# Next batch's input tile by tile, GpSimd's pivot step first, and every loop over batches written out

## The chip, the cores and the metric

One core of one Trainium2 chip runs the whole program in one launch. The metric is the device time of the launch in microseconds, the median of several runs. Engines: TensorE (matmuls), VectorE, ScalarE, GpSimd (POOL) and SyncE (SP), each with its own instruction stream; they meet at semaphores.

## The reference

The input x is (8, 512, 576), the condition (8, 576), all float32:

```
ada = silu(c) @ W_ada + b_ada       # shift, scale, gate for attention and for the MLP
h = layernorm(x) * (1 + scale_msa) + shift_msa
x = x + gate_msa * (softmax(q * 36**-0.5 @ k.T) @ v @ W_proj + b_proj)    # 16 heads of 36
h = layernorm(x) * (1 + scale_mlp) + shift_mlp
x = x + gate_mlp * (gelu(h @ W_fc1 + b_fc1) @ W_fc2 + b_fc2)              # 2304 wide
U, _ = qr(P)                                   # P is (576, 64)
R = expm(skew(silu(c) @ W.T + b))              # one 64x64 rotation a batch
z = x @ U;  out = x + (z @ R - z) @ U.T
```

## The kernel before, in words

A first block loads and splits the weights. Each float32 matrix is held as a rounded high part and a low part, and products are sums of three passes (high x high, high x low, low x high).

The attention block works through the 8 batches, each in 64 numbered slots: 4 slots a head, one for each 128 keys. In slot n TensorE issues the scores for the row maximum of slot n + 10 (L1025), the scores for slot n + 2 (L1041), then the "units" that a hand-written table FIRST_SLOT puts in this slot, then the value products of slot n (L1052, L1053). ScalarE takes two exponentials a slot (phi, L741, and pf, L744), VectorE the row maximum of slot n + 9 (L868) and the low part plo of slot n (L875). The units share two PSUM banks G in turn: `ln` transposes a fifth of the next batch's normalised x (L940), `qk` and `v` are the projections of the next heads, `tr` and `p` transpose and project the output of the batch before, `rv` computes rows of the rotation, and `el` broadcasts a row of the pivot matrix (L1003).

The pivot matrix serves the QR of P: an elimination of 64 steps in batches 0 to 3 and another of 64 in batches 4 to 7, one step for each head. For head h TensorE broadcasts the row (unit el h), VectorE copies it to prow (L856), and GpSimd does the step: `cholesky_step` in batches 0 to 3 (L582 to L593), `sign_step` in batches 4 to 7 (L620 to L635). el h + 1 waits for step h through row_ready. GpSimd does step h in slot 4h + 3.

The next batch's x goes into one tile xln of 4 token tiles, which also holds the residual of the batch before until its rows are stored (L675, for tiles 0 to 3 in slots 13, 20, 24 and 31). GpSimd loads the whole of it in slot 32 (L242). VectorE takes the statistics of tile i in slot 36 + i (L249, L252), GpSimd the inverse root of the variance of all four in slot 39 (L258, L260), VectorE normalises in slots 40 and 41 (L265). TensorE transposes in slots 41 to 45. For the part transposed in slot n, VectorE modulates in slot n + 1 (L813), ScalarE copies the high part in slot n + 2 (L706), and VectorE subtracts for the low part in slot n + 2 (L821), which frees the bank for slot n + 2's transposes.

Within a slot GpSimd's order is: divide the head's output, add and store the residual, load x, invert, load the residual, pick rows for the pivots, pivot step. In slot 39 the inversion thus stands ahead of pivot step 9, which reads what VectorE copied in slot 38, and which el 10 in slot 40 waits for.

Batches -1 (only the preparation of batch 0), 0, 7 and 8 (only the last output) are written out in each engine's stream. Between them run loops with a register for b: on TensorE, VectorE and GpSimd one over batches 1 to 3 and one over 4 to 6, on ScalarE and SyncE one over 1 to 6. Waits in a loop compare with values computed from the register. A third block computes the rotations; the last one, the MLP, works in 16 chunks of 256 tokens, two a batch, with a loop over batches 1 to 6 on every engine.

## Time and profile before

| what | value |
|---|---|
| three runs | 2677.41 us median (2676.99 to 2680.6) |
| the profiled execution | 2683.11 us, span 2681.5 us |
| mean granted TensorE clock | 0.944 of full speed |
| busy share | TensorE 88%, VectorE 53%, ScalarE 41%, GpSimd 29% |
| start | to 128.5 us (el 0 of batch 0) |
| attention, el 0 of batch 0 to the end | 128.5 to 1499 us |
| rotations | 1499 to 1624 us |
| MLP | 1624 to the end |

A span is from the first to the last instruction. A row of a timeline gives start, duration (us), engine, line, operation, what is written and read, and in brackets the idle time before it with what ended it; "issue" means that the profile shows nothing that the engine waited for. A row of windows gives the stretch, its length, then busy time and (x instructions) of TensorE, of its weight loads, of VectorE, ScalarE and GpSimd, the granted TensorE clock as a share of full speed (1.0 is 2.4 GHz, 0.5 is 1.2 GHz), the mean busy share of the DMA engines, and GB/s. Waits give the total in us, how many, and the longest. "el h" is the L1003 of head h, and a window between two of them is taken from start to start.

### The profile page before, as it was taken

The page shows a single profiled execution, that of the slowest core. Times are in us where ns is not written, and L with a number is a line of the kernel's source. Part 1 is how long each engine was busy: PE and PEld are TensorE (multiplying, and loading weights), DVE is VectorE, ACT ScalarE, POOL GpSimd, SP SyncE. Part 2 cuts the span into 40 slices and gives each one's busy share as a digit, 9 for nine tenths or more (in the row PEclk, how much of TensorE's full clock was granted, in tenths as well). Part 3 has the DMA queues.
Part 4 walks back from the last instruction along what each step waited for, and adds up shares of the span by engine and source line. Part 5 has one row for each costly group of instructions (what it writes and reads, how often), then busy time and mean ns, then how long its engine had stood idle before and what let it go on. Part 6 is the DMA issues. An engine that isn't in the chain of part 4 may idle for free. (4 is left out here: it accounts for less than half of the span.)

```text
span 2681.5 us, 49135 instructions
## 1 busy us (share of the span) xinstructions
PE 2365.1 (88%) x15081; PEld 2036.1 (76%) x15081; DVE 1428.6 (53%) x2994; ACT 1098.9 (41%) x2362; POOL 766.5 (29%) x1547
## 2 busy tenths in 40 slices
PE   6698988988889789898997468999999999999998
PEld 1466756756667577576774457999999999999998
DVE  3577676676776767767776473333333333333332
ACT  2265555555555555555655122222222222222221
POOL 1033333343434344334445481111111111111110
PEclk9798999989999899899998688999999999999998
DMA  7122222231322222222221241010101010110100
GB/s 227 38 75 72 56 81 70 64 91 51 88 68 59 72 73 85 70 55 80 72 71 54 70 129 40 28 39 28 39 27 39 28 39 31 35 37 30 36 26 27
DMA packets 99893, 160.53 MB, mean 60 GB/s; under 512 B 23296, under 2 KB 43872, under 8 KB 99616
## 3 DMA queue, kind: packets, MB, share of 16 engines
q1 hardware_dynamic: 86752, 110.35, 14.4%
q0 software_dynamic: 11856, 46.60, 5.3%
q8 instruction: 143, 2.34, 0.4%
q14 instruction: 118, 0.97, 0.1%
q10 hardware_dynamic: 1024, 0.26, 0.0%
HBM read 80.10 MB, written 20.16 MB: 37 GB/s over the span
## 5 line engine op out<-in xcount | busy, mean ns | idle before, releaser
L1653 PE MATMUL bank<-h2T,w 128*128 128x256 f32 x4032 | 531.0, 283 | 9.7 <-issue 6.9
L1653 PEld LDWEIGHTS bank<-h2T,w 128*128 128x128 f32 x4032 | 508.0, 191 | 11.3 <-issue 8.1
L1562 DVE TENSOR_TENSOR glo<-bank,ghi 128x256 fp32r<-128x256 f32 x288 | 122.2, 424 | 688.5 <-ACT bank L1529 688.5
L1666 PE MATMUL bank<-w,ghi 128*128 128x288 f32 x2304 | 476.5, 298 | 0.4
L1528 ACT ACTIVATE ghi<-bank,b 128x256 fp32r<-128x256 f32 x288 | 136.4, 474 | 689.4 <-PE bank L1653 689.4
L875 DVE TENSOR_TENSOR plo<-pf,phi 128x512 fp32r<-128x512 f32 x512 | 365.3, 713 | 89.0 <-ACT pf L744 86.1
L868 DVE TENSOR_REDUCE negm<-bank 128x1 f32<-128x512 f32 x512 | 349.3, 683 | 108.9 <-PE bank L1025 103.6
L1666 PEld LDWEIGHTS bank<-w,ghi 128*128 128x128 f32 x2304 | 367.2, 189 | 2.4 <-DVE x2T L1572 2.0
L741 ACT ACTIVATE phi<-bank 128x512 fp32r<-128x512 f32 x512 | 307.6, 601 | 94.5 <-PE bank L1041 58.8
L1666 PE MATMUL bank<-w,glo 128*128 128x288 f32 x1152 | 340.8, 296 | 0.0
L744 ACT ACTIVATE pf<-bank 128x512 f32<-128x512 f32 x512 | 310.0, 605 | 0.2 <-DVE plo L875 0.2
L960 PE MATMUL bank<-hT,wqk 128*128 128x512 f32 x1008 | 261.5, 399 | 2.9 <-DVE hT L821 2.9
L1052 PE MATMUL bank<-phi,vv 128*73 128x512 f32 x512 | 227.2, 444 | 36.2 <-DVE plo L875 35.4
L1025 PE MATMUL bank<-ks,qs 108*128 108x512 f32 x512 | 235.4, 460 | 18.0 <-issue 11.8
L1041 PE MATMUL bank<-qs,ks 109*128 109x512 f32 x512 | 218.7, 427 | 19.3 <-ACT pf L744 13.0
L960 PEld LDWEIGHTS bank<-hT,wqk 128*128 128x128 f32 x1008 | 192.1, 191 | 47.6 <-DVE hT L821 3.3
L1666 PEld LDWEIGHTS bank<-w,glo 128*128 128x128 f32 x1152 | 216.4, 188 | 0.0
L1053 PE MATMUL bank<-plo,vv 128*73 128x512 f32 x512 | 211.3, 413 | 0.0
L948 PEld LDWEIGHTS bank<-wv,hT 128*128 128x128 f32 x896 | 135.4, 198 | 35.4 <-DVE qklo L833 19.9
L948 PE MATMUL bank<-wv,hT 128*128 128x288 f32 x896 | 147.8, 309 | 11.1 <-DVE qklo L833 10.3
L1502 POOL TENSOR_TENSOR xs<-xs,x2T 128x288 f32<-128x288 f32 x64 | 49.5, 807 | 360.5 <-DVE x2T L1572 360.5
L1025 PEld LDWEIGHTS bank<-ks,qs 108*128 108x128 f32 x512 | 102.2, 200 | 64.7 <-issue 27.0
(222 smaller groups left out, 3300.4 us busy)
## 6 DMA issues: line engine op xcount, KB each, us to landing
xln<-x POOLq DMA_DIRECT2D x16, 1152.0 KB, 6.7
qs<-qkhi SPq DMA_DIRECT2D x192, 72.0 KB
ks<-qkhi SPq DMA_DIRECT2D x192, 72.0 KB
wst<-w_fc POOLq DMA_DIRECT2D x34, 288.0 KB, 3.1
x_d<-xln POOLq DMA_DIRECT2D x32, 288.0 KB, 2.5
xa<-x_d SPq DMA_DIRECT2D x32, 288.0 KB, 2.7
xs<-x_d SPq DMA_DIRECT2D x16, 576.0 KB, 4.0
out<-xs SPq DMA_DIRECT2D x16, 576.0 KB, 2.9
```

What stands on the lines that cost most here:

```text
L741: act.activation(phi[PBUF[n]][:, :], S[n % 2][:, :], ACT.Exp, scale=SCALE).then_inc(exp_hi, 1)
L744: act.activation(pf[n % 2][:, :], S[n % 2][:, :], ACT.Exp, scale=SCALE).then_inc(exp_f, 1)
L868: dve.tensor_reduce(negm[m // TT % 2][:, m % TT:m % TT + 1], M[m % 2][:, :], AX.X, ALU.max, negate=True).then_inc(m_read, 1)
L875: dve.tensor_tensor(plo[PBUF[n]][:, :], pf[n % 2][:, :], f32(phi[PBUF[n]][:, :]), ALU.subtract).then_inc(p_lo, 1)
L948: mm = pe.matmul(G[g_bank(it, u)][:, 0:HALF], hT[0:rows, a, tt * PAR:(tt + 1) * PAR], wv[0:rows, w, half * HALF:(half + 1) * HALF], start= ...
L960: mm = pe.matmul(G[g_bank(it, u)][:, :], wqk[0:rows, w, t * PAR:(t + 1) * PAR], hT[0:rows, a, :], start=first, stop=last)
L1025: pe.matmul(M[m % 2][:, :], qs[h % RING][0:STACK, qt * PAR:(qt + 1) * PAR], ks[h % RING][0:STACK, :], start=True, stop=True).then_inc(m_fu ...
L1041: pe.matmul(S[m % 2][:, :], ks[h % RING][:, kt * PAR:(kt + 1) * PAR], qs[h % RING][:, :], start=True, stop=True).then_inc(s_full, 1)
L1052: pe.matmul(O[0:2 * HD + 1, :], v, phi[PBUF[n]][:, :], start=(kt == 0), stop=False)
L1053: pe.matmul(O[0:2 * HD + 1, :], v, plo[PBUF[n]][:, :], start=False, stop=(kt == TT - 1)).then_inc(pv, 1)
L1653: mm = pe.matmul(F[ft % 2][:, 0:CH], w1[0:rows, w, ft * PAR:(ft + 1) * PAR], h[0:rows, a, :], start=(i == 0), stop=(i == len(FULL_PASSES) ...
L1666: mm = pe.matmul(Y[2 * tt + half][:, 0:HALF], g[ft % 2][:, span], w2[:, ft, w, half * HALF:(half + 1) * HALF], start=(ft == 0 and i == 0), ...
```

## The change

All loops over batches are written out, in the attention block and in the MLP block; waits then compare with constants. x of the next batch is loaded in four transfers, each with its own semaphore and each waiting for the store of its own tile, and statistics, inversion and normalisation are spread over earlier slots. In a slot GpSimd does the pivot step ahead of the inversion and the loads; step 9 moves from slot 39 to slot 38, el 0 from slot 1 to 2, el 11 from slot 47 to 46. Modulate, the high copy and the low subtraction each come one slot earlier relative to their transposes.

```
@@ -86,18 +86,21 @@
               (43, ("ln", 2)), (44, ("ln", 3)), (45, ("ln", 4)), (48, ("qk", 0)), (50, ("v", 0, 0)), (52, ("qk", 1)),
               (54, ("v", 0, 1)), (57, ("v", 0, 2)), (59, ("qk", 2)), (61, ("v", 0, 3)), (10, ("rv", 0)), (18, ("rv", 1)), (30, ("rv", 2)), (56, ("rv", 3))]
 RV = 4
-BROADCAST_SLOT = {h: TT * h + 1 for h in range(HEADS)} | {10: 40, 11: 47}
+BROADCAST_SLOT = {h: TT * h + 1 for h in range(HEADS)} | {0: 2, 10: 40, 11: 46}
 FIRST_SLOT = sorted(FIRST_SLOT + [(_n, ("el", _h)) for _h, _n in BROADCAST_SLOT.items()], key=lambda at: (at[0], at[1][0] != "el"))
 IN_ONE_SLOT = [("v", 1, 2), ("v", 1, 3), ("p", 0, 1), ("p", 1, 0), ("p", 2, 0), ("p", 2, 1)]
 TR_SLOT = [_n for _n, _u in FIRST_SLOT if _u[0] == "tr"]
 assert all(_n % TT == TT - 1 for _n in TR_SLOT)
 MAX_LEAD = 10
-STAT_SLOT, INVERT_SLOT, NORM_SLOT = 36, 39, 40
-LOAD_SLOT, RESIDUAL_SLOT = 32, 48
+LOAD_AT = {16: 0, 23: 1, 27: 2, 33: 3}
+STAT_AT = {20: 0, 27: 1, 31: 2, 36: 3}
+INVERT_AT = {33: (0, 3), 37: (3, 4)}
+LN_NORM_AT = {34: 0, 35: 1, 37: 2, 39: 3}
+RESIDUAL_SLOT = 48
 EARLY = 5
 EARLY_SLOT = 28
 ACT_LAG, DVE_LAG = 1, 1
-ELIM_SLOT = {TT * _h: _h for _h in range(HEADS)}
+STEP_SLOT = {(38 if _h == 9 else TT * _h + 3): _h for _h in range(HEADS)}
 
 
 def shift(unit):
@@ -213,7 +216,8 @@
         mv = sb(attn, "mv", [PAR, TT, 2])
         rstd = sb(attn, "rstd", [PAR, 2, TT])
         mhalf = sb(attn, "mhalf", [PAR, TT])
-        x_in, st_done, mv_done = sem("x_in"), sem("st_done"), sem("mv_done")
+        x_in = [sem(f"x_in{i}") for i in range(TT)]
+        st_done, mv_done = sem("st_done"), sem("mv_done")
         rstd_step, ln_norm = sem("rstd_step"), sem("ln_norm")
         stages = ExitStack()
         cond = sb(stages, "cond", [PAR, KT + 1, BATCH])
@@ -237,31 +241,32 @@
 
         xb = x.rearrange("b (t p) c -> b p t c", p=PAR)
 
-        def load_x(engine, b):
-
-            engine.dma_start(xln[:, :, :].unsqueeze(1), xb[bass.ds(b, 1)].rearrange("o p t c -> p o t c")).then_inc(x_in, 16)
+        def load_x(engine, b, tt):
+
+            engine.dma_start(xln[:, tt, :].unsqueeze(1), xb[bass.ds(b, 1), :, tt, :].rearrange("o p c -> p o c")).then_inc(x_in[tt], 16)
 
         def statistics(dve, b, tt):
 
-            if tt == 0:
-                dve.wait_ge(x_in, 16 * (b + 1))
+            dve.wait_ge(x_in[tt], 16 * (b + 1))
             for half in range(2):
                 dve.bn_stats(stats[:, tt, half, :], xln[:, tt, half * HALF:(half + 1) * HALF]).then_inc(st_done, 1)
             dve.wait_ge(st_done, (b * TT + tt + 1) * 2)
             alone(dve)
             dve.bn_aggr(mv[:, tt, :], stats[:, tt, :, :]).then_inc(mv_done, 1)
 
-        def invert(pool, b):
-
-            pool.wait_ge(mv_done, TT * (b + 1))
+        def invert(pool, b, part):
+
+            first, end = part
+            done = 4 * b + (2 if first else 0)
+            pool.wait_ge(mv_done, TT * b + end)
             alone(pool)
-            pool.tensor_scalar(rstd[:, 0, :], mv[:, :, 1], LN_EPS, None, ALU.add).then_inc(rstd_step, 1)
-            pool.wait_ge(rstd_step, 2 * b + 1)
-            pool.tensor_tensor(rstd[:, 1, :], rstd[:, 0, :], mhalf[:, :], ALU.pow).then_inc(rstd_step, 1)
+            pool.tensor_scalar(rstd[:, 0, first:end], mv[:, first:end, 1], LN_EPS, None, ALU.add).then_inc(rstd_step, 1)
+            pool.wait_ge(rstd_step, done + 1)
+            pool.tensor_tensor(rstd[:, 1, first:end], rstd[:, 0, first:end], mhalf[:, first:end], ALU.pow).then_inc(rstd_step, 1)
 
         def normalise(dve, b, tt):
 
-            dve.wait_ge(rstd_step, 2 * b + 2)
+            dve.wait_ge(rstd_step, 4 * b + (4 if tt == TT - 1 else 2))
             dve.tensor_scalar(xln[:, tt, :], xln[:, tt, :], mv[:, tt, 0:1], rstd[:, 1, tt:tt + 1],
                               ALU.subtract, ALU.mult).then_inc(ln_norm, 1)
 
@@ -287,7 +292,8 @@
 
             @block.gpsimd
             def _(pool):
-                load_x(pool, 0)
+                for tt in range(TT):
+                    load_x(pool, 0, tt)
                 pool.memset(ident[:, :], 0.0).then_inc(const_ready, 1)
                 pool.memset(below[:, :], 0.0).then_inc(const_ready, 1)
                 pool.memset(dcol[:, :], 0.0).then_inc(const_ready, 1)
@@ -308,7 +314,8 @@
                     rows = PAR if t < KT else REM
                     pool.dma_start(stage[i % 3][0:rows, 0:n], src[t * PAR:t * PAR + rows, :]).then_inc(stage_in[i % 3], 16)
                     if i == 2:
-                        invert(pool, 0)
+                        for part in INVERT_AT.values():
+                            invert(pool, 0, part)
 
             @block.scalar
             def _(act):
@@ -463,7 +470,8 @@
         early_moved = sem("early_moved")
         ax_full, ax_free = sem("ax_full"), sem("ax_free")
         a_hi = sem("a_hi")
-        gate_in, r_in, xo_done, x1_out = sem("gate_in"), sem("r_in"), sem("xo_done"), sem("x1_out")
+        gate_in, r_in, xo_done = sem("gate_in"), sem("r_in"), sem("xo_done")
+        x1_out = [sem(f"x1_out{i}") for i in range(TT)]
         fixed = sem("fixed")
         elim, picked, row_ready = sem("elim"), sem("picked"), sem("row_ready")
         wrot_in = sem("wrot_in")
@@ -472,32 +480,17 @@
 
         def run(engine, slot):
 
-            for b in (-1, 0):
+            for b in range(-1, BATCH + 1):
                 for n in range(SLOTS):
                     slot(b, n)
-            with engine.Fori(1, BATCH - 1) as b:
+
+        def run_phases(engine, slot, between=None):
+
+            for b in range(-1, BATCH + 1):
+                if b == BATCH // 2 and between is not None:
+                    between()
                 for n in range(SLOTS):
-                    slot(b, n)
-            for b in (BATCH - 1, BATCH):
-                for n in range(SLOTS):
-                    slot(b, n)
-
-        def run_phases(engine, slot, between=None):
-
-            for b in (-1, 0):
-                for n in range(SLOTS):
-                    slot(b, n, 0)
-            with engine.Fori(1, BATCH // 2) as b:
-                for n in range(SLOTS):
-                    slot(b, n, 0)
-            if between is not None:
-                between()
-            with engine.Fori(BATCH // 2, BATCH - 1) as b:
-                for n in range(SLOTS):
-                    slot(b, n, 1)
-            for b in (BATCH - 1, BATCH):
-                for n in range(SLOTS):
-                    slot(b, n, 1)
+                    slot(b, n, int(b >= BATCH // 2))
 
         def pivot_matrix(phase, h):
 
@@ -636,17 +629,18 @@
                     pool.wait_ge(elim, base + 9)
                     pool.sem_inc(row_ready, 1)
 
-                def load_next_x(b):
+                def load_next_x(b, tt):
                     if not isinstance(b, int) or b >= 2:
-                        pool.wait_ge(x1_out, 16 * TT * (b - 1))
-                    load_x(pool, b)
+                        pool.wait_ge(x1_out[tt], 16 * (b - 1))
+                    load_x(pool, b, tt)
 
                 def load_residual(b):
 
                     if not isinstance(b, int) or b < BATCH - 1:
                         pool.wait_ge(g_full, g_use(b, ("ln", KT)) + 1)
                     if isinstance(b, int) and b == BATCH - 1:
-                        pool.wait_ge(x1_out, 16 * TT * b)
+                        for tt in range(TT):
+                            pool.wait_ge(x1_out[tt], 16 * b)
                     pool.dma_start(xln[:, :, :].unsqueeze(1), xb[bass.ds(b, 1)].rearrange("o p t c -> p o t c")).then_inc(r_in, 16)
                     if not isinstance(b, int) or b >= 1:
                         pool.wait_ge(g_free, g_use(b, ("p", TT - 1, 1)) + 3)
@@ -672,7 +666,7 @@
                     pool.wait_ge(g_free, g_use(it, ("p", qt, 1)) + 3)
                     pool.tensor_tensor(xln[:, qt, :], xln[:, qt, :], xo[qt % 2][:, :], ALU.add).then_inc(xo_done, 1)
                     pool.wait_ge(xo_done, b * TT + qt + 3)
-                    pool.dma_start(x1b[bass.ds(b, 1), :, qt, :].rearrange("o p c -> p o c"), xln[:, qt, :].unsqueeze(1)).then_inc(x1_out, 16)
+                    pool.dma_start(x1b[bass.ds(b, 1), :, qt, :].rearrange("o p c -> p o c"), xln[:, qt, :].unsqueeze(1)).then_inc(x1_out[qt], 16)
 
                 def slot(b, n, phase):
                     if n % TT == 3 and is_there(b, n - TT):
@@ -680,19 +674,20 @@
                     for _, qt, half in [u for u in units(b, ENDS_AT.get(n - 2, [])) if u[0] == "p"]:
                         if half == 1:
                             add_x(b - 1, b, qt)
-                    if n == LOAD_SLOT and has_next(b):
-                        load_next_x(b + 1)
-                    if n == INVERT_SLOT and has_next(b):
-                        invert(pool, b + 1)
+                    if n == 0 and is_there(b, 0):
+                        pick_rows(b, phase)
+                    if n in STEP_SLOT and is_there(b, 0):
+                        (sign_step if phase else cholesky_step)(b, STEP_SLOT[n])
+                    if n in INVERT_AT and has_next(b):
+                        invert(pool, b + 1, INVERT_AT[n])
+                    if n in LOAD_AT and has_next(b):
+                        load_next_x(b + 1, LOAD_AT[n])
                     if n == RESIDUAL_SLOT and is_there(b, 0):
                         load_residual(b)
-                    if n == 0 and is_there(b, 0):
-                        pick_rows(b, phase)
-                    if n - 3 in ELIM_SLOT and is_there(b, 0):
-                        (sign_step if phase else cholesky_step)(b, ELIM_SLOT[n - 3])
 
                 run_phases(pool, slot, turn_to_signs)
-                pool.wait_ge(x1_out, 16 * TT * BATCH)
+                for tt in range(TT):
+                    pool.wait_ge(x1_out[tt], 16 * BATCH)
 
             @block.scalar
             def _(act):
@@ -780,10 +775,9 @@
                         move_mrow(b, (n + 4) // TT)
                     if n == EARLY_SLOT and is_there(b, 0):
                         move_early(b)
-                    for u in units(b, ENDS_AT.get(n - ACT_LAG - 1, [])):
+                    for u in units(b, ENDS_AT.get(n - ACT_LAG, [])):
                         if u[0] == "ln":
                             hT_his(b, u[1])
-                    for u in units(b, ENDS_AT.get(n - ACT_LAG, [])):
                         if u[0] == "v":
                             v_his(b, u[1], u[2])
                         if u[0] == "qk":
@@ -892,9 +886,12 @@
                         p_los(b, n)
                     if n % TT == 2 and is_there(b, n - TT):
                         read_o(b, n)
+                    for u in units(b, ENDS_AT[n]):
+                        if u[0] == "ln":
+                            modulate(b, u[1])
                     for u in units(b, ENDS_AT.get(n - DVE_LAG, [])):
                         if u[0] == "ln":
-                            modulate(b, u[1])
+                            hT_los(b, u[1])
                         if u[0] == "v":
                             v_los(b, u[1], u[2])
                         if u[0] == "qk":
@@ -907,14 +904,10 @@
                             take_row(b, u[1], phase)
                         if u[0] == "rv":
                             take_rotation(b, u[1])
-                    for u in units(b, ENDS_AT.get(n - DVE_LAG - 1, [])):
-                        if u[0] == "ln":
-                            hT_los(b, u[1])
-                    if STAT_SLOT <= n < STAT_SLOT + TT and has_next(b):
-                        statistics(dve, b + 1, n - STAT_SLOT)
-                    if NORM_SLOT <= n < NORM_SLOT + TT // 2 and has_next(b):
-                        normalise(dve, b + 1, 2 * (n - NORM_SLOT))
-                        normalise(dve, b + 1, 2 * (n - NORM_SLOT) + 1)
+                    if n in STAT_AT and has_next(b):
+                        statistics(dve, b + 1, STAT_AT[n])
+                    if n in LN_NORM_AT and has_next(b):
+                        normalise(dve, b + 1, LN_NORM_AT[n])
 
                 run_phases(dve, slot)
 
@@ -1436,11 +1429,9 @@
             chunk(-1, NC - 1)
             for j in range(NC):
                 chunk(0, j)
-            with engine.Fori(1, BATCH - 1) as b:
+            for b in range(1, BATCH):
                 for j in range(NC):
                     chunk(b, j)
-            for j in range(NC):
-                chunk(BATCH - 1, j)
             chunk(BATCH, 0)
 
         with nc.Block() as block:
```

## Rows read from the trace of the kernel before

**Rows 1.** Windows between el 15 and the next el 0, at four of seven joints

```profile
272.70:282.04 9.34, 8.63 (x52) 7.02 (x51) 7.77 (x15) 5.77 (x13) 3.65 (x10) 1.00 0.29 81
...
441.51:458.95 17.44, 11.39 (x52) 9.32 (x51) 8.69 (x17) 6.23 (x13) 3.98 (x10) 0.80 0.19 49
...
793.57:807.07 13.50, 10.17 (x53) 8.34 (x52) 8.82 (x17) 6.11 (x13) 4.76 (x13) 0.87 0.21 57
...
1316.38:1325.94 9.56, 8.57 (x52) 7.00 (x51) 7.87 (x15) 5.99 (x13) 4.16 (x12) 1.00 0.29 79
```

**Rows 2.** Timeline of TensorE at the end of the turn of batch 1

```profile
449.55 0.49 PE L1025 MATMUL bank<-ks,qs 108*128 108x512 f32 x1 [2.76 <-issue]
...
453.00 0.58 PE L1041 MATMUL bank<-qs,ks 109*128 109x512 f32 x1 [2.96 <-issue]
```

**Rows 3.** Timeline of GpSimd at the same end of turn

```profile
451.02 0.71 POOL L571 COPY pick<-ident 128x16 f32 x1 [3.41 <-issue]
```

**Rows 4.** Windows between el 9 and el 12, batches 0, 1, 4, 7

```profile
208.51:245.24 36.73, 25.26 (x104) 17.47 (x103) 28.96 (x56) 18.99 (x38) 12.10 (x26) 0.77 0.13 37
...
377.50:413.56 36.06, 24.65 (x104) 16.71 (x103) 30.10 (x58) 18.98 (x37) 11.58 (x26) 0.81 0.14 38
...
901.53:940.21 38.68, 25.65 (x104) 16.78 (x103) 30.65 (x60) 19.65 (x39) 13.02 (x32) 0.78 0.13 36
...
1419.06:1445.17 26.11, 17.82 (x71) 10.74 (x69) 18.25 (x35) 16.39 (x33) 12.65 (x30) 0.87 0.18 50
```

**Rows 5.** Timeline of TensorE, el 10 of batch 1

```profile
388.51 0.77 PE L1003 MATMUL bank<-chol,pick 128*128 128x128 f32 x2 [5.16 <-POOLq L595]
```

**Rows 6.** Timeline of GpSimd before el 10 of batch 1

```profile
383.36 0.23 POOL L258 TENSOR_SCALAR rstd<-mv 128x4 f32<-128x4 f32 x1 [3.84 <-DVE mv L252]
...
384.70 0.67 POOL L582 TENSOR_TENSOR small<-prow,small 64x1 f32<-64x1 f32 x1
...
387.73 0.45 POOL L593 TENSOR_TENSOR chol<-chol,carry 64x127 f32<-64x127 f32 x1
```

**Rows 7.** Timeline of VectorE, the row copy for step 9 of batch 1

```profile
379.59 0.27 DVE L856 COPY prow<-bank 64x128 f32<-64x128 f32 x1
```

**Rows 8.** Windows between el 0 and el 9, in batches 1 and 7

```profile
282.04:377.50 95.46, 89.24 (x498) 70.11 (x497) 67.79 (x133) 54.38 (x112) 37.58 (x81) 1.00 0.27 78
...
1325.94:1419.06 93.12, 88.33 (x497) 69.88 (x496) 67.33 (x130) 54.45 (x112) 41.84 (x98) 1.00 0.24 67
```

**Rows 9.** Waits of the whole span: total us, times, longest

```profile
ACT phi L741 <- issue: 19.4, 32, 2.6
```

**Rows 10.** Windows of two MLP chunks each, with an end of turn and without

```profile
2348.75:2479.41 130.66, 129.15 (x1034) 128.68 (x1033) 41.10 (x108) 35.44 (x92) 16.42 (x21) 1.00 0.11 34
...
2479.41:2608.34 128.93, 128.93 (x1035) 128.66 (x1033) 40.96 (x108) 35.44 (x92) 16.42 (x21) 1.00 0.10 32
```

**Rows 11.** Timeline of VectorE, a pair of statistics and normalisations, batch 1

```profile
379.79 0.80 DVE L249 BATCH_NORM_STATS2 stats<-xln 128x6 f32<-128x288 f32 x2
...
380.69 0.21 DVE L252 BATCH_NORM_AGGREGATE mv<-stats 128x2 f32<-128x12 f32 x1
...
384.75 1.07 DVE L265 TENSOR_SCALAR xln<-xln,mv,rstd 128x576 f32<-128x576 f32 x2 [0.34 <-POOL rstd L260]
```

**Rows 12.** Window between el 9 and el 10 in batch 7

```profile
1419.06:1425.85 6.79, 3.57 (x17) 2.07 (x15) 4.81 (x9) 5.67 (x11) 4.32 (x10) 0.92 0.22 62
```

**Rows 13.** Waits of the whole span, TensorE for the low parts of hT

```profile
PE bank L940 <- DVE hT L821: 27.9, 17, 1.8
```

**Rows 14.** DMA issues of the page: count, KB each, median us to landing

```profile
xln<-x POOLq DMA_DIRECT2D x16, 1152.0 KB, 6.7
...
wst<-w_fc POOLq DMA_DIRECT2D x34, 288.0 KB, 3.1
```

**Rows 15.** Timeline of GpSimd at the start, fourth weight load

```profile
27.40 0.63 POOL L309 DMA_DIRECT2D stage<-w_qk  x1 [5.07 <-DVE wqk L347]
```

**Rows 16.** DMA queues of the page: packets, MB, share of 16 engines

```profile
q8 instruction: 143, 2.34, 0.4%
```

## Prediction

> **What bounds the kernel now.** I read the windows between the pivot broadcasts first, since L1003 is issued once per head, at a fixed slot, and so works as a milestone of the 64 slots of a batch. I call the L1003 of head h "el h". Before the change el 0 is in slot 1, el 9 in slot 37, el 10 in slot 40, el 12 in slot 49 and el 15 in slot 61. The attention stage from el 0 of batch 0 to its end is some 1370 of 2681.5 us and goes at about 174 us for a batch; the MLP stage takes about 1060 us with TensorE nearly full. Neither is stopped by one engine throughout: in both the question is at which places TensorE stands still.
>
> Three kinds of place stand out, and the change touches all of them.
>
> First, the step from one batch to the next. Between el 15 and the next el 0 lie 9.34 us where the two batches are written out one after the other (0 to 1) and 9.56 us at 6 to 7, but 13.50 to 17.44 us at the five ends of a turn of a loop [rows 1]. At such an end TensorE stands idle twice, 2.76 and 2.96 us, and both are put down to "issue": no other engine is named [rows 2]. GpSimd has the same gap, 3.41 us, before its first instruction of the turn [rows 3]. Each engine sits at its own jump back, and one that arrives later stalls the others again. The granted clock of the longest such window is 0.80 where it is 1.00 at the written-out joints [rows 1], so part of the 8 us is TensorE at the lower of its levels after the gap.
>
> Second, the stretch from el 9 to el 12, in which the next batch's input is normalised and transposed. It takes 36.06 to 38.68 us in the seven batches that prepare a next one (three of them shown), and 26.11 us in batch 7, which does not [rows 4]. In it TensorE waits 5.16 us for el 10, and for GpSimd [rows 5]. GpSimd has waited 3.84 us for the last statistics, has then done the addition and the 1.05 us power of L260, and only then starts the pivot step that el 10 needs, 384.70 to 388.18 [rows 6]. The row copy that the step reads was due already at 379.59 [rows 7]. So the step was ready to run about 4.8 us before it ran.
>
> Third, little delays in the turns of a loop. From el 0 to el 9, batch 7 (written out) takes 93.12 us and batch 1 95.46 us with as many instructions on TensorE within two [rows 8]; ScalarE has 32 idle pieces, 19.4 us, before L741 that nothing but "issue" explains [rows 9]. In the MLP stage two chunks take 128.93 us where written out and 130.66 us with an end of turn in them, TensorE busy 129 us in both [rows 10].
>
> **The change part by part.**
>
> *Loops written out, attention.* The five windows that hold an end of turn add up to 17.44 + 16.40 + 13.50 + 13.94 + 14.54 = 75.82 us (two of the five are shown in [rows 1]). At the written-out joints' 9.45 us each they would be 47.25. Gain 28.6 us. The instructions executed are the same, since a turn is itself some thousand instructions written one after the other and shows no such gap within. Bounds: 24 (the first TensorE gaps and their echo, without the clock) to 29. The turn to signs at batch 4 stays; its GpSimd work is hidden today and el 0 comes one slot later, so I add nothing. The Trainium skill's page "Runtime: NRT & Kernel Launch", section "Instruction fetch mechanics", has the rule that a taken branch out of the fetched window must wait for a fetch; it also says that running straight on over a block's end is mostly hidden. The rows above agree with the first half; the second bears on the last rival.
>
> *Loops written out, waits with constants.* Batches 1 to 6 take 569.9 us from el 0 to el 9, and 6 x 93.12 is 558.7: at most 11.2 us. Batch 7 lacks the x load, so not all of it need be the registers. I take 9; bounds 0 to 11.2.
>
> *Loops written out, MLP.* Five pairs of chunks at a mean of 130.57 us against 128.93, 8.2 us, from rows like [rows 10]. TensorE is the bound there and nothing fills the gap. I take 8.1; bounds 6.7 (the pieces of idle time alone) to 9.
>
> *GpSimd's pivot step first, statistics early.* Step 9 moves to slot 38, the inversion is split (slots 33 and 37), three of four statistics go to slots 20, 27, 31, and the normalisations to 34, 35, 37, 39. The stretch el 9 to el 12 holds 30.10 us of VectorE work in batch 1 [rows 4]. Two statistics (0.80 us for the pair of L249 and 0.21 for L252, 1.03 with their spacing) and two normalisations (1.07 for a pair) [rows 11] leave it: 30.1 - 2.1 - 1.0 = 27.0 us. VectorE will not be gapless. The step still takes 3.5 us after the copy, so el 9 to el 10 comes to about 6.3 us (2.1 to the copy, 0.3 for it, 3.5, 0.3 to TensorE), and batch 7 shows just this with nothing else in the way: 6.79 us [rows 12]. A wait of some 2.4 us is left there, which also idles VectorE. Add 0.6 for the first modulate, which waits for its transposes. 27.0 + 3.0 = 30.0 us, against a mean of 259.44 / 7 = 37.06: 7.0 us, times seven 49 us. The statistics also stop waiting for x. Modulate and the low-part subtraction each move one slot earlier, so TensorE's waits for L821, 17 of up to 1.8 us [rows 13], shrink; that is inside the 30.0. Bounds: 3.6 a batch (25 us; the pivot wait is halved, and the rest of the stretch refills to its old length) and 9.0 (63 us; 28.1 us, nearly VectorE's floor).
>
> *What the moved work costs where it lands.* Three statistics and two normalisations a batch are 3 x 1.03 + 2 x 0.53 = 4.1 us of VectorE in slots 20, 27, 31, 34, 35. In 20 and 31 TensorE does two parts of a projection or half a qk tile and is the slower; around 34 VectorE is nearly the bound. If the cover were gone everywhere it would be 29 us; I take 0.4 a batch, 3 us. Bounds 0 to 8.
>
> *x in four transfers.* One of 1152 KB lands in 6.7 us, transfers of 288 KB on the same queue in 3.1 [rows 14]. Tiles are loaded in slots 16, 23, 27, 33 and read in 20, 27, 31, 36; a slot lasts 2 to 3 us, so the tightest has 3 slots. Each load waits for the store of the same tile of the batch before, issued 3 slots ahead for tiles 0 to 2 and two for tile 3. GpSimd stands in order: behind a late store would queue the head's division and pivot step 8. It is busy for 29% of the span and on the path only at el 10, hence 0. The Trainium skill's page "SBUF — State Buffer", section "The DMA setup-cost knee", says to merge transfers because of a fixed cost near 2 us each, which speaks against this part: by it four tiles would take about 6 us more of queue time a batch than one load. No engine waits for the sum of the four.
>
> *Start of the program.* GpSimd issues four x loads instead of one and does two inversions. Weight loads come up to 2 us later, into 5.07 us that GpSimd waits before the fourth today [rows 15]. I take +1, bounds 0 to 3.
>
> Sum: 49 + 28.6 + 9 + 8.1 - 3 - 1 = 90.7 us. The profiled execution itself took 2683.1 (span 2681.5), so 2592.4 for its like. The runs' median 2677.4 lies 5.7 lower; from it, 2587.
>
> **Rivals.**
>
> *Refilled stretch.* The transposes, modulate, ScalarE copy and subtraction form a chain through two banks. If it keeps its length, el 9 to el 12 gives only the pivot part: 25 instead of 49 us, 2611. For it: today's waits for L821 [rows 13] lie within the chain itself. Against: they come from the order in the slots, which is changed.
>
> *Both go better.* Shorter gaps keep the granted clock up (0.77 to 0.81 in the stretch today [rows 4]), the stretch comes to 28.1 us, registers give all of 11.2, nothing is paid back: 111 us, about 2567.
>
> *The written-out loops do not do what they say.* The fetch waits turn up elsewhere, say where one engine's code is read on while others load data. Then 28.6 + 8.1 are lost: 54 us gained, 2623. Against it: none at the joints 0 to 1 and 6 to 7.
>
> *Slower.* The engines' code is brought by two queues, the larger with 143 packets [rows 16]. If running on over a packet's end stopped TensorE for the 2.9 us of a jump, 32 such stops would eat the whole 90.7 us; one packet in four, 36 stops, makes 104 us and 2691. Today's program already crosses them in its long turns without a gap, so this is improbable. By the section of the Trainium skill's page on instruction fetch named above, such ends are mostly hidden and this rival would not occur.
>
> **Chances.** Forecast 0.62, refilled stretch 0.18, both better 0.14, loops without effect 0.04, slower 0.02. The range 2566 to 2613 takes in the first three, each in part, and leaves out 2 in 10. The likeliest one's own range is 2578 to 2598. A measurement of this kernel tells changes of over 0.2% (5 us). Faster: all but the last and a part of unforeseen mishaps, 0.97; same 0.01; slower 0.02.
>
> **What would show it.** Right: all seven windows el 15 (slot 61) to el 0 (now slot 2, so one slot of about 2 us longer) without a TensorE gap put to issue; GpSimd's L571 without its 3.4 us; TensorE's wait for el 10 at 2 to 3 us, no longer behind L260; el 9 to el 12 near 30 us; pairs of chunks at 128.9. Wrong: VectorE waiting for x at L249, above all tile 3; a longer el 0 to el 9 in batches 1 to 6 than 94 us; the stretch still over 33 us; new issue gaps at regular distances.

## The result, and the profile after

The changed kernel takes 2612.02 us (median of four runs, 2607.42 to 2613.68) where the kernel before took 2679.01 beside it (four runs, 2676.99 to 2683.96): ratio 0.9733, 95% interval 0.9711 to 0.9755. A later comparison gave 0.9745 (0.9727 to 0.9764). So it is faster, by 67 us. The forecast was 2587: the time lies 25 us above it, at the upper end of the range of 2566 to 2613 and outside the likeliest case's own range of 2578 to 2598.

The profiled execution took 2613.1 us. The page of the changed kernel, its span, the busy times and the instruction queue:

```profile
span 2611.3 us, 43520 instructions
...
PE 2348.9 (90%) x15081; PEld 2023.5 (77%) x15081; DVE 1424.7 (55%) x2994; ACT 1100.5 (42%) x2362; POOL 807.3 (31%) x1587
...
q8 instruction: 121, 1.98, 0.3%
```

Written-out loops did not bring more instruction packets (121, [rows 16] had 143). Five windows follow: the joint el 15 to el 0 after batch 1, the stretch el 9 to el 12 in batches 1 and 3, el 0 to el 9 in batch 1, and two chunks of the MLP.

```profile
432.11:442.36 10.25, 9.53 (x56) 7.72 (x55) 8.56 (x18) 6.50 (x15) 3.79 (x10) 1.00 0.28 78
371.05:404.35 33.30, 25.18 (x104) 16.47 (x103) 25.33 (x48) 19.12 (x37) 13.07 (x26) 0.85 0.17 43
700.14:731.73 31.59, 23.16 (x104) 14.72 (x103) 25.23 (x48) 19.12 (x37) 12.59 (x26) 0.95 0.16 43
277.86:371.05 93.19, 87.82 (x492) 69.64 (x491) 71.56 (x140) 53.69 (x111) 42.99 (x88) 1.00 0.28 79
2275.00:2403.93 128.93, 128.93 (x1035) 128.65 (x1033) 40.91 (x108) 35.51 (x92) 16.43 (x22) 1.00 0.12 34
```

The joint that took 17.44 us [rows 1] takes 10.25, one slot more included, and so do the other six (10.25 to 10.38). The MLP pair is at the 128.93 us of the written-out pair of [rows 10]. The stretch came down from 36 to 39 us [rows 4] to 31.6 to 33.7, not to 30.0; its VectorE work is 25.2 to 25.3 us, less than the 27.0 forecast (one normalisation is left in it, where the forecast left two), so VectorE stands idle in it for 6 to 8 us and not for 3. El 0 to el 9 lost its first slot and yet is only 2.3 us shorter than in [rows 8], and 5.0 us shorter in batches 1 to 6 together.

Between el 9 and el 10 lies the step that matters. Timelines of the changed kernel, batch 3: TensorE at el 10, GpSimd's pivot step 9, and VectorE at the same time.

```profile
707.37 0.35 PE L996 MATMUL bank<-chol,pick 128*128 128x128 f32 x1 [2.95 <-POOLq L588]
...
702.17 0.54 POOL L575 TENSOR_TENSOR small<-prow,small 64x1 f32<-64x1 f32 x1 [2.69 <-DVE prow L850]
702.69 1.05 POOL L576 TENSOR_TENSOR small<-prow,pick 64x1 f32<-64x1 f32 x1
703.92 1.02 POOL L579 TENSOR_SCALAR small<-chol,small,lower 64x1 f32<-64x1 f32 x1 [0.18 <-POOL small L576]
704.90 0.18 POOL L580 TENSOR_TENSOR dcol<-dcol,small 64x1 f32<-64x1 f32 x1
705.26 0.65 POOL L583 TENSOR_SCALAR carry<-prow,small 64x127 f32<-64x127 f32 x1 [0.17 <-POOL dcol L580]
705.85 0.69 POOL L584 COPY chol<-small 64x1 f32<-64x1 f32 x1
706.62 0.44 POOL L586 TENSOR_TENSOR chol<-chol,carry 64x127 f32<-64x127 f32 x1
...
702.52 0.67 DVE L869 TENSOR_TENSOR plo<-pf,phi 128x512 fp32r<-128x512 f32 x1
703.12 0.57 DVE L270 TENSOR_SCALAR xln<-xln,mv,rstd 128x576 f32<-128x576 f32 x1
703.61 0.68 DVE L862 TENSOR_REDUCE negm<-bank 128x1 f32<-128x512 f32 x1
704.21 0.67 DVE L869 TENSOR_TENSOR plo<-pf,phi 128x512 fp32r<-128x512 f32 x1
...
710.97 0.82 DVE L807 TENSOR_SCALAR bank<-bank,adaT 128x512 f32<-128x512 f32 x1 [4.46 <-PE bank L933]
```

The step no longer waits for the inversion; it starts 0.17 us after its copy. But it takes 4.89 us (702.17 to 707.06) and not the 3.5 of before [rows 6]. L576, one element in each of 64 partitions, takes 1.05 us; the same operation takes 0.18 elsewhere. It ends 0.05 us after VectorE's L270, the normalisation, and L579 ends 0.06 us after the low part plo. The step of before ran beside normalisations too (L265, [rows 11]), yet the operation like L576 took 0.18 there:

```profile
385.20 0.18 POOL L583 TENSOR_TENSOR small<-prow,pick 64x1 f32<-64x1 f32 x1
```

What is new is that the step starts right behind its copy, where it meets two plo in a row, one of them with a normalisation behind it. TensorE waits 2.95 us meanwhile, and VectorE then 4.46 us for TensorE's transposes.

Where the 70.2 us of span went, by sums of the windows between broadcasts: from el 0 of batch 0 to el 0 of batch 7 59.4, in the MLP 8.2, in batch 7 3.1, start 0.4, rotations 1.8; the end of the attention stage and the change to the next block cost 2.7.

### The profile page after: what moved, and what is told of

Same layout as the page of the kernel before. It is cut to its first block and busy times, and to the rows that moved or that the text cites. A ratio compares the mean times of both kernels' runs of the same rounds, so it can differ in the third digit from the quotient of the medians.

```text
span 2611.3 us, 43520 instructions
## 1 busy us (share of the span) xinstructions
PE 2348.9 (90%) x15081; PEld 2023.5 (77%) x15081; DVE 1424.7 (55%) x2994; ACT 1100.5 (42%) x2362; POOL 807.3 (31%) x1587
## 5 line engine op out<-in xcount | busy, mean ns | idle before, releaser
L869 DVE TENSOR_TENSOR plo<-pf,phi 128x512 fp32r<-128x512 f32 x512 | 372.4, 727 | 80.0 <-ACT pf L739 77.5
L862 DVE TENSOR_REDUCE negm<-bank 128x1 f32<-128x512 f32 x512 | 347.7, 679 | 77.6 <-PE bank L1018 75.3
L953 PE MATMUL bank<-hT,wqk 128*128 128x512 f32 x1008 | 267.6, 406 | 2.9 <-DVE hT L815 2.9
L1045 PE MATMUL bank<-phi,vv 128*73 128x512 f32 x512 | 221.2, 432 | 48.7 <-DVE plo L869 47.8
L953 PEld LDWEIGHTS bank<-hT,wqk 128*128 128x128 f32 x1008 | 197.7, 196 | 50.9 <-DVE hT L815 3.3
L941 PE MATMUL bank<-wv,hT 128*128 128x288 f32 x896 | 142.5, 302 | 10.6 <-DVE qklo L827 9.9
L941 PEld LDWEIGHTS bank<-wv,hT 128*128 128x128 f32 x896 | 128.9, 189 | 28.7 <-DVE qklo L827 21.1
L986 PE MATMUL bank<-wp,aT 128*128 128x288 f32 x832 | 131.2, 303 | 20.6 <-DVE vv L821 7.3
```

What stands on the lines that cost most here:

```text
L862: dve.tensor_reduce(negm[m // TT % 2][:, m % TT:m % TT + 1], M[m % 2][:, :], AX.X, ALU.max, negate=True).then_inc(m_read, 1)
L869: dve.tensor_tensor(plo[PBUF[n]][:, :], pf[n % 2][:, :], f32(phi[PBUF[n]][:, :]), ALU.subtract).then_inc(p_lo, 1)
L941: mm = pe.matmul(G[g_bank(it, u)][:, 0:HALF], hT[0:rows, a, tt * PAR:(tt + 1) * PAR], wv[0:rows, w, half * HALF:(half + 1) * HALF], start= ...
L953: mm = pe.matmul(G[g_bank(it, u)][:, :], wqk[0:rows, w, t * PAR:(t + 1) * PAR], hT[0:rows, a, :], start=first, stop=last)
L1045: pe.matmul(O[0:2 * HD + 1, :], v, phi[PBUF[n]][:, :], start=(kt == 0), stop=False)
```

## The experiments

Ratios are against the kernel before on the same chip (median 2681.61 for the first four, 2681.99 for the next four, 2681.12 for the last four); in brackets the 95% interval. Sums over seven batches are batches 0 to 6, over six batches 1 to 6.

### Each half alone

The kernel before with its loops written out and its order untouched:

```
-            for b in (-1, 0):
-            with engine.Fori(1, BATCH - 1) as b:
-            for b in (BATCH - 1, BATCH):
+            for b in range(-1, BATCH + 1):
```

> The kernel before with all loops over batches written out, its order in the slots untouched. Theory A (the loop part is worth what the windows at the ends of a turn and the MLP pairs showed): el 15 to el 0 at about 9.4 us everywhere instead of 13.5 to 17.4, MLP pairs at 128.9 us, no idle piece put to issue before L741; gain 28.6 + 8.2 + up to 9, so 38 to 46 us, 2633 to 2641. The stretch el 9 to el 12 stays at 36 to 38.7 us. Rival B (only the idle pieces at the jump themselves go, and what follows them is refilled): 2 x 2.9 us at each of two ends and 3 at the other three, 6.7 in the MLP, 27 us, about 2652.

Measured: 2625.55 us, 0.9793 (0.9771 to 0.9814), 55 us gained (50 to 61), more than expected.

And the changed kernel with the loops back in:

```
-            for b in range(-1, BATCH + 1):
+            with engine.Fori(1, BATCH - 1) as b:
```

> The changed kernel with the loops over batches put back as they were. Theory A (the two parts add): gain 72 minus the written-out part's 38 to 46, so 26 to 34 us, 2645 to 2653; el 9 to el 12 near 32.6 us as in the changed kernel, ends of turn at 14 to 18 us. Rival B (the orders of the slots only pay where the waits compare with constants): under 20 us.

Measured: 2670.96 us, 0.9965 (0.995 to 0.9979), 9 us gained, so the expected 26 to 34 fell. The order's effect on top of written-out loops is 0.9733 or 0.9745 against 0.9793, 13 to 16 us, so 9 to 16 us in all; the forecast had 45. Windows of the kernel with loops alone written out, the joint after batch 1, el 0 to el 9 of batch 2 and the stretch of batch 3:

```profile
437.97:447.30 9.33, 8.62 (x52) 7.01 (x51) 7.68 (x15) 5.76 (x13) 3.79 (x10) 1.00 0.29 79
...
447.30:540.07 92.77, 88.67 (x498) 70.12 (x496) 68.00 (x133) 54.36 (x112) 38.05 (x81) 1.00 0.28 79
704.79:741.65 36.86, 25.35 (x104) 17.52 (x103) 29.60 (x58) 18.86 (x38) 12.11 (x26) 0.77 0.13 37
```

All seven joints take 9.3 us, the five former ends of turn 46.7 against 75.8: 29.2. El 0 to el 9 takes 92.7 to 92.8 in each of batches 1 to 6, 13.4 us less in all, more than the 11.2 of the forecast's own bound. The MLP gives 8.2. A further 1.5 us came off the stretch and 2.7 off el 12 to el 15, over seven batches. With loops back in, the new order's end of turn after batch 1 takes 17.77 us, clock 0.81:

```profile
433.74:451.51 17.77, 11.46 (x56) 9.24 (x55) 8.79 (x18) 6.94 (x15) 3.92 (x10) 0.81 0.19 50
```

### Registers: ScalarE's and SyncE's loop alone

The kernel before with only the attention loop of ScalarE and SyncE written out:

```
+        def run_written_out(engine, slot):
+            for b in range(-1, BATCH + 1):
+                for n in range(SLOTS):
+                    slot(b, n)
...
-                run(act, slot)
+                run_written_out(act, slot)
```

> The kernel before with the attention loop of ScalarE and SyncE alone written out; TensorE, VectorE, GpSimd and the MLP keep their loops. Theory A (the short pauses inside the turns are ScalarE's, the idle pieces put to issue before L741): el 0 to el 9 of batches 1 to 6 falls from 94.5 to 95.5 us to 92.8, as in e1_written_out; the ends of turn keep the 13 us of those with one gap less, some 3 us shorter each; gain 11 + 10, about 2660. Rival B (the pauses belong to the waits on registers of TensorE and VectorE): the windows stay at 94.5, gain under 8 us.

Measured: 2662.78 us, 0.9927 (0.991 to 0.9943), 20 us gained.

```profile
281.04:374.01 92.97, 88.71 (x497) 70.06 (x496) 67.60 (x132) 54.31 (x112) 37.78 (x81) 1.00 0.28 79
```

El 0 to el 9 of batches 1 to 6 sums to 556.8 against 569.9, the same 13 us as with all loops written out, though TensorE, VectorE and GpSimd still compare with registers. The waits of ScalarE that only "issue" explains [rows 9] are gone. So this term belongs to the two streams with the written-out loop, and by those waits probably to ScalarE. TensorE, VectorE and GpSimd pay nothing measurable for register waits here.

Whether ScalarE's term is the comparison with a register is not shown. Its short idle pieces in the loop of before come 8 to 12 us apart for the most part, and at changing lines:

```profile
288.62 0.41 ACT L714 ACTIVATE vv<-bank 128x288 fp32r<-128x288 f32 x1 [0.20 <-issue]
299.78 0.60 ACT L731 ACTIVATE aT<-bank 128x512 fp32r<-128x512 f32 x1 [0.22 <-issue]
```

That would also fit something that depends on how much code has gone by, and writing the loop out takes away both.

Of the ends of turn only 5 us went, and 4.1 of them at one place, the step from batch 3 to 4. There only ScalarE and SyncE had a jump back, since the loops of the other three end at it. That step took 13.50 us in the kernel before [rows 1] and takes 9.38 here:

```profile
782.61:791.99 9.38, 8.67 (x52) 6.97 (x51) 7.80 (x15) 5.77 (x13) 5.42 (x13) 1.00 0.30 81
```

So leaving one loop and entering the next costs the other engines nothing measurable, and at the four other ends the jumps back of these three keep the step long, whatever ScalarE does.

### The old lags, and el 10 later

The changed kernel with modulate, high copy and low subtraction one slot later again, and el 11 in slot 47:

```
-                    for u in units(b, ENDS_AT.get(n - ACT_LAG, [])):
+                    for u in units(b, ENDS_AT.get(n - ACT_LAG - 1, [])):
                         if u[0] == "ln":
                             hT_his(b, u[1])
```

> The changed kernel with modulate, high copy and low subtraction back at one slot later (and el 11 in slot 47, which their order needs). Theory A (the earlier lags are part of the gain: VectorE ran the transposes' slots gapless at 2.52 us each in the changed kernel, and waited 0.2 to 0.8 us in each before): 1 to 2 us a batch back, 7 to 14 us slower than the changed kernel, 2619 to 2626; TensorE waits for L815 of 1 to 1.8 us again. Rival B (the pivot step and the early statistics are all of it): within 3 us of the changed kernel's 2612.

Measured: 2607.08 us, 0.9732 (0.971 to 0.9753), not slower as was expected. Run again later beside the changed kernel:

> The changed kernel with the old lags once more, to size the difference. If the earlier lags of the change cost time (el 10 to el 12 as the traces have it, 0.6 us a batch in seven batches): 4 to 6 us less than the changed kernel beside it, 0.15 to 0.25%. If the first comparison was chance: within 2 us of it.

> The changed kernel once more, on the same chip as the runs beside it: 2608 to 2614 us. It is the yardstick for the next run.

Measured: 2607.06 us, 0.9716 (0.9699 to 0.9734), with the old lags, and 2614.0, 0.9745, for the changed kernel. The intervals overlap; the difference of 7 us agrees with the windows, where el 12 to el 15 takes 27.2 us instead of 27.8 in each of seven batches and el 9 to el 12 is 2.3 us shorter in all. So the earlier lags gave nothing, and probably cost some 5 us. They moved a wait: between el 10 and el 12 TensorE waits 4.0 us a batch for the low-part subtraction of hT with the old lags, and with the new ones 1.1 us for it but 3.3 for plo. A row of the changed kernel:

```profile
726.23 0.45 PE L1045 MATMUL bank<-phi,vv 128*73 128x512 f32 x1 [0.95 <-DVE plo L869]
```

The changed kernel with el 10 in slot 46 and the later broadcasts every three slots:

```
-BROADCAST_SLOT = {...} | {0: 2, 10: 40, 11: 46}
+BROADCAST_SLOT = {...} | {0: 2, 10: 46, 11: 49, 12: 52, 13: 55, 14: 58, 15: 61}
```

> The changed kernel with el 10 in slot 46 instead of 40 and el 11 to 15 every third slot behind it (49, 52, 55, 58, 61), steps two slots after each. TensorE then has no pivot row to wait for between el 9 and the transposes. Theory A (what kept the stretch at 32.6 us instead of 30 is the wait of 2.9 to 3.5 us left at el 10, with the lower clock behind it and VectorE standing for 4.5 us at the first modulate): 3 to 4.5 us a batch, 21 to 32 us, 2580 to 2591. Rival B (the stretch is VectorE's and ScalarE's chain anyway; the wait turns up at the modulates): under 1 us a batch, 2605 to 2612. Rival C (pivot steps every third slot come too fast, TensorE waits at el 11 to 15 instead): slower than 2612.

Measured: 2606.1 us, 0.9729 (0.9706 to 0.9753). The wait for GpSimd at el 10 is gone; what stands there is 0.23 us for VectorE:

```profile
717.63 0.46 PE L996 MATMUL bank<-chol,pick 128*128 128x128 f32 x2 [0.23 <-DVE hT L815]
...
734.18 1.90 PE L953 MATMUL bank<-hT,wqk 128*128 128x512 f32 x7 [0.94 <-DVE vv L821]
745.21 1.26 PE L1005 MATMUL bank<-siluT,wrot 128*128 128x8 f32 x10 [1.26 <-DVE vv L821]
```

In batch 3 el 9 to slot 46 shrank from 22.6 to 18.4 us, but slots 46 to 61, which now hold six broadcasts instead of five with their copies and steps, grew from 36.8 to 42.1, with waits for VectorE. So the wait was paid for elsewhere, and theory A fell. That the crowded copies are what made the later slots longer is argued from these waits and was not tried by itself.

### Is the wait for el 10 on the path?

The changed kernel with four unused powers added to pivot step 9:

```
+                    if h == 9:
+                        for i in range(4):
+                            pool.tensor_tensor(spare[:, i:i + 1], prow[:, 0:1], minus1[:, :], ALU.pow)
```

> The changed kernel with four more powers (about 0.56 us each on GpSimd, results unused) at the start of pivot step 9, so the row that el 10 waits for comes 2.2 us later. Theory A (TensorE's wait at el 10 is on the path: each us of it is a us of time): 7 x 2.2 = 15 us slower than the changed kernel, a few more for the clock, 2627 to 2632; the wait at el 10 grows from 2.9 to 5.1 us. Rival B (the stretch el 9 to el 12 is set by VectorE's work, the wait only fills room): under 5 us slower.

Measured: 2627.13 us, 0.9789 (0.9773 to 0.9806), 12 to 15 us more than the changed kernel.

```profile
717.51 0.77 PE L1003 MATMUL bank<-chol,pick 128*128 128x128 f32 x2 [4.60 <-POOLq L592]
```

The four powers made the step 1.65 us longer in batches 0 to 3, not 2.2. The wait grew from 2.95 to 4.60 us, and el 9 to el 10 by 11.0 us over seven batches, as much as the seven steps did. The runs differ by 12 to 15, so nothing of it was hidden: what lengthens step 9 costs its own length.

### Lighter slots for the statistics

The old lags, with the statistics of tiles 0 and 1 and the normalisations moved to other slots:

```
-STAT_AT = {20: 0, 27: 1, 31: 2, 36: 3}
+STAT_AT = {25: 0, 29: 1, 31: 2, 36: 3}
-LN_NORM_AT = {34: 0, 35: 1, 37: 2, 39: 3}
+LN_NORM_AT = {35: 0, 37: 1, 39: 2, 40: 3}
```

> e3_old_lags with the statistics of tiles 0 and 1 moved from slots 20 and 27 to 25 and 29, in which VectorE has only its row maximum and low part, and the normalisations from 34, 35, 37, 39 to 35, 37, 39, 40. Theory A (the early VectorE work is paid where it lands: TensorE waits 1.0 to 1.3 us for L821 after slot 20 and 1.1 us for the low part of slot 34, the last with a lower clock behind it in some batches): 1.3 to 2.5 us a batch back, 9 to 17 us faster than e3_old_lags, 2590 to 2598; el 5 to el 6 at 12.6 instead of 13.4 to 13.9 us, el 8 to el 9 at 9.2 instead of 9.7. Rival B (these windows are longer for x loads and stores at their new places): unchanged within 4 us.

Measured: 2613.55 us, 0.9738 (0.9721 to 0.9755), not faster than the version it was built on. The expectation fell. The surplus at el 5 to el 6 went (12.55 us instead of 13.4), and came back at el 6 to el 7 (9.64 instead of 9.2) and el 7 to el 8 (10.3 instead of 9.3). And step 9 became longer, 5.50 us in batches 0 to 3. Neither of the two placements tried between slots 20 and 40 lets VectorE take them for nothing.

### The step first, nothing else

The kernel with its loops written out and its old order, but GpSimd's step ahead of the inversion and the loads, and step 9 in slot 38. x comes in one transfer and the statistics stay in slots 36 to 39:

```
-ELIM_SLOT = {TT * _h: _h for _h in range(HEADS)}
+STEP_SLOT = {(38 if _h == 9 else TT * _h + 3): _h for _h in range(HEADS)}
```

> e1_written_out with two edits of the change only: GpSimd's pivot step ahead of its other work in a slot, and step 9 in slot 38. x comes in one transfer, statistics, inversion and normalisations are where they were before. Theory A (the pivot row was what TensorE waited for, so this alone takes most of what the order gave, and none of what the moved VectorE work cost): el 10's wait falls from 5.1 to about 3 us; 2 to 3 us a batch, 14 to 21 us faster than e1_written_out, 2605 to 2612, as fast as the whole change. Rival B (with the step first, the inversion and the normalisations become late and TensorE waits for them at the first transposes instead): within 5 us of e1_written_out.

Measured: 2614.86 us, 0.9748 (0.9732 to 0.9765), within its interval as fast as the whole change. Its el 0 to el 9 of batch 3 and its stretch:

```profile
605.98:698.76 92.78, 88.75 (x498) 70.13 (x497) 68.35 (x134) 54.38 (x112) 38.06 (x81) 1.00 0.28 79
698.76:731.80 33.04, 24.66 (x104) 16.23 (x103) 29.20 (x57) 19.44 (x38) 11.57 (x26) 0.85 0.15 41
```

Step 9 takes 3.2 us here in batches 0 to 3, and TensorE waits 0.26 us at most for GpSimd at el 10, since TensorE itself is held up before (1.77 us for plo). El 9 to el 12 is 34.6 us on the mean against 32.6 in the changed kernel: two of VectorE's statistics and all normalisations are still in it. The surplus is behind el 10, where el 10 to el 12 takes 28.4 us on the mean and TensorE now waits for the normalisation as well; in batch 3:

```profile
704.34:731.80 27.46, 21.10 (x88) 14.12 (x89) 23.86 (x44) 15.84 (x31) 8.68 (x19) 0.82 0.12 33
```

But el 0 to el 9 keeps its 92.8 us. The two come out even: moving statistics and normalisations forward gave 14 us in the stretch and cost about as much where they landed.

### Without statistics, and with the normalisation on ScalarE

Two kernels on the version with the old lags (e12 above, 2607.06). The first leaves out statistics, inversion and normalisation for the batches after the first; x is transposed as it comes in:

```
-                    if n in STAT_AT and has_next(b):
-                        statistics(dve, b + 1, STAT_AT[n])
-                    if n in LN_NORM_AT and has_next(b):
-                        normalise(dve, b + 1, LN_NORM_AT[n])
...
-                    if n in INVERT_AT and has_next(b):
-                        invert(pool, b + 1, INVERT_AT[n])
```

> The kernel with the lags as before (2607.1 us, span 2606.1) without the statistics, the inverse root and the normalisation of the batches after the first: their rows of x are multiplied as they come in. It bounds what all the moved VectorE work together costs. Theory A (that work is on the path wherever it is put): el 5 to el 6 falls from 13.4 to 12.6 us, el 8 to el 9 from 9.7 to 9.2, together 1.3 us a batch, and el 9 to el 12 loses another 0.5 to 1 us: 12 to 16 us in all, 2591 to 2595 us. Rival B (only its landing just ahead of a copy costs, and the rest is hidden): 7 to 9 us, from the windows before el 9 alone, about 2599 us. Rival C (the surplus of these windows comes from the transfers of x or the clock): under 4 us, above 2603 us.

The second computes all of it, but ScalarE normalises, with the scale and bias that GpSimd prepares in two more small operations:

```
+        def normalise_on_act(act, b, tt):
+            act.wait_ge(rstd_step, 8 * b + (8 if tt == TT - 1 else 4))
+            act.activation(xln[:, tt, :], xln[:, tt, :], ACT.Identity, bias=rstd[:, 3, tt:tt + 1],
+                           scale=rstd[:, 1, tt:tt + 1]).then_inc(ln_norm, 1)
...
-LN_NORM_AT = {34: 0, 35: 1, 37: 2, 39: 3}
+LN_NORM_AT = {36: 0, 37: 1, 38: 2, 40: 3}
```

> The kernel with the lags as before (2607.1 us, span 2606.1) with the normalisation of the next batch's four tiles moved from VectorE to ScalarE, in slots 36, 37, 38 and 40; GpSimd makes two more small operations for it per part. Theory A (statistics and normalisation cost time because they sit on VectorE ahead of a copy that TensorE waits for): the waits of 1.13 us near slot 34 go, el 8 to el 9 falls from 9.7 to 9.2 us and el 9 to el 12 loses up to 0.7 us, together 5 to 8 us over seven batches: 2599 to 2602 us. Rival B (ScalarE is as tight as VectorE in these slots, because TensorE waits for the exponentials there, which now come 0.65 us later): the window el 9 to el 10 grows by what el 8 to el 9 loses: 2605 to 2612 us.

Measured: 2588.38 us, 0.9655 (0.9636 to 0.9674), without; 2591.49 us, 0.9668 (0.9648 to 0.9688), with the normalisation on ScalarE. Both gains are larger than expected. The second kernel gives 15.6 us over its base and 22.5 over the changed kernel, and is the fastest here that computes everything. The stretch and its part el 9 to el 10 in batch 3, step 9 and el 10 of this kernel:

```profile
691.97:722.02 30.05, 22.80 (x105) 15.66 (x103) 25.44 (x47) 20.37 (x40) 10.15 (x24) 0.89 0.16 45
...
691.97:697.63 5.66, 3.79 (x17) 2.10 (x15) 4.89 (x10) 5.25 (x10) 3.00 (x8) 1.00 0.27 77
...
694.00 0.54 POOL L584 TENSOR_TENSOR small<-prow,small 64x1 f32<-64x1 f32 x1 [2.88 <-DVE prow L862]
694.52 0.18 POOL L585 TENSOR_TENSOR small<-prow,pick 64x1 f32<-64x1 f32 x1
694.89 0.63 POOL L588 TENSOR_SCALAR small<-chol,small,lower 64x1 f32<-64x1 f32 x1 [0.19 <-POOL small L585]
...
696.44 0.35 POOL L593 COPY chol<-small 64x1 f32<-64x1 f32 x1
...
697.63 0.35 PE L1006 MATMUL bank<-chol,pick 128*128 128x128 f32 x1 [1.08 <-POOLq L597]
```

The operation that took 1.05 us takes 0.18, the step 3.33 us instead of 4.89, the wait at el 10 1.08 instead of 2.95, and el 9 to el 10 5.66 instead of 7.23. In batches 4 to 6 the step takes 4.0 us instead of 5.4. Over seven batches el 9 to el 10 is 41.6 us against 51.8 in the changed kernel, 10.2 us, and the seven steps alone are 10.3 us shorter (25.3 against 35.6). El 9 to el 12 is 30.2 us on the mean, the forecast's 30.0. El 8 to el 9 is back at 9.2 us from 9.7.

The first kernel tells how much of that is the normalisation. With nothing of it anywhere, step 9 still takes 3.87 us in batches 0 to 3, and 4.50 in batches 4 to 6, as in batch 7 of the changed kernel; its L579 takes 1.02 us beside plo. So the normalisation makes about 1.0 us of the 4.89. The other 0.55 us that the kernel with ScalarE's normalisation gains go with a plo that starts 0.27 us later against the step and lets the operation like L576 through ahead of it, a matter of timing that the edit did not aim at.

It also shows what is left of el 10 to el 12. With none of the work on VectorE that part still takes 24.6 us on the mean; in the kernel before it took 25.4, in the changed one 25.2, with ScalarE's normalisation 24.3. TensorE waits there mostly for the low-part subtraction of hT, 3.4 us a batch in the kernel before and 4.0 with none of the work. Batch 3 of the kernel without it, and one such wait:

```profile
692.21:716.93 24.72, 19.58 (x88) 13.92 (x89) 20.30 (x37) 14.02 (x28) 7.35 (x17) 0.87 0.13 36
...
704.23 0.63 PE L928 MATMUL bank<-ident,xln 128*128 128x128 f32 x4 [1.68 <-DVE hT L814]
```

So against the kernel before about 1 us a batch was to be gained in this part by taking work off VectorE. The work is not free everywhere: with the step first and the work left where it was, the part took 28.4.

## Why the prediction was right and wrong, point by point

The sum was 90.7 us; of span 70.2 were gained. The time lies in the range, 1 us from its end. Two parts of the sum were far too good, the stretch by 18 us and the moved work by 6 to 11; the waits with constants gave 4 us more than forecast and took some of that back.

- **Ends of turn** (28.6): right, 29.2 by the kernel with the loops alone written out.
- **Waits with constants** (9, bounds 0 to 11.2): the size was too small, 13.4, beyond the bound. The bound took batch 7's 93.12 us [rows 8] for the length without registers; batches 1 to 6 come to 92.7 to 92.8. Only ScalarE's and SyncE's loops matter; that it is their waits is not shown.
- **MLP** (8.1): right, 8.2.
- **The stretch** (49): wrong, 31.0 (259.4 to 228.4 over seven batches). This is the failed step, "27.0 + 3.0 = 30.0 us". It took VectorE's busy time as the floor; that fell to 25.3, further than forecast, and the stretch did not follow. The gain at the pivot was right in kind: el 9 to el 10 fell from 81.4 to 51.8 us. But "The step still takes 3.5 us after the copy" was taken from the step of before, which ran at another moment and in batches 0 to 3 alone (3.9 in 4 to 6); right behind its copy it took 4.9 and 5.4. The window of batch 7, on which the forecast leaned, holds a step of 4.50 us. Together el 9 to el 10 is 7.7 us of the miss (51.8 against seven times 6.3), of which the kernel without statistics and normalisation gives back 6.6. The rest, 10.7 us, is el 10 to el 12, forecast at 23.7 and measured at 25.2, where 25.4 had been, and 24.6 with all of the work gone. By TensorE's waits for hT it is bound by the chain that the rival *refilled stretch* names, transposes, modulate, copy and subtraction through two banks; that is read from the waits, and no run changed the chain apart from its lags. The rival priced this at 25 us and 2611. That the time came to 2612 is in part luck, since the stretch gave 31, the waits 4 more than forecast, and the moved work took that back.
- **What the moved work costs** (3, bounds 0 to 8): wrong, 9 to 14 us. The changed kernel's 564.9 us for el 0 to el 9 in batches 1 to 6 stand against 556.5 with the old order, which has one slot of 0.93 us more in each: 564.9 - (556.5 - 5.6) = 14.0. Three windows at a lower clock are in it, of 1.5 us each; the kernel with the old lags, whose order is the same up to el 9, had none in its first profile and took 560.3, so 9.4. The kernel without the work is 18.7 us faster than its base and the one with ScalarE's normalisation 15.6. Slot 20, which I had called covered by TensorE, shows TensorE waiting for VectorE behind the statistics; the last row is the wait behind slot 34's normalisation:

```profile
657.23 0.80 DVE L252 BATCH_NORM_STATS2 stats<-xln 128x6 f32<-128x288 f32 x2
...
659.42 0.45 DVE L821 TENSOR_TENSOR vv<-bank,vv 128x288 fp32r<-128x288 f32 x1
...
659.92 2.00 PE L986 MATMUL bank<-wp,aT 128*128 128x288 f32 x13 [1.01 <-DVE vv L821]
694.68 0.42 PE L1045 MATMUL bank<-phi,vv 128*73 128x512 f32 x1 [1.15 <-DVE plo L869]
```

- **The earlier lags**, counted inside the 30.0: no gain, probably a loss of 5 us.
- **x in four transfers** (0) **and the start** (1): no wait for x at the statistics. 288 KB landed in 3.5 us, so four in 14.0 by their sum against 6.7 for one of 1152 KB, and nothing waited for it. El 0 of batch 0 came at 128.1 us, 0.4 earlier, but at 130.5 in the second profile of the same kernel, so the start tells nothing. Moving the load of x alone was not tried.
- **Loops without effect, and slower**: neither came. There are no issue gaps at regular distances.

What stays open: whether the windows at a lower clock come from the moved work (below). How far ScalarE's normalisation gives its gain by the shorter step and how far by VectorE's free time is known from windows (10.2 us at el 9 to el 10, the rest elsewhere), not from a kernel with one of them alone; its normalisations also stand in other slots. The step's own length is shown to act one to one.

## What to carry to other kernels

Before work is moved off a crowded stretch, ask what bounds each part of it. Here VectorE was busy for most of the stretch, but the gain over the kernel before came at the pivot wait, and the work taken out cost about as much in the slots where it landed. When you move a chain of small GpSimd operations, price it beside the VectorE operations that it will then meet, not by its length at its old place. Where VectorE's work can be taken by ScalarE, try that before moving it about on VectorE; here it gave 16 us. Writing a long loop out paid at every end of turn on the path and within ScalarE's turns, and the window of the loop against its written-out neighbour told the first of these to within 1 us.
